# Gathering the first edge pass's rows of x during the first node pass, through a table by edge

## What is computed

```python
h = jnp.maximum(_layernorm(x, axis=-1), 0.0)
x = x + _L0_gnn_ref(src, dst, h, L0_gnn_W, L0_gnn_b)
h = jnp.maximum(_layernorm(x, axis=-1), 0.0)
x = x + _L1_gnn_ref(h, edge_index, edge_attr_4, edge_attr_16, ...)
```

```python
deg = 1.0 + jax.ops.segment_sum(jnp.ones((E,), X.dtype), col, num_segments=N)
dinv = jax.lax.rsqrt(deg)
XW = X @ W + b
scaled = XW * dinv[:, None]
msg = jax.ops.segment_sum(scaled[col], row, num_segments=N)
out = (msg + scaled) * dinv[:, None]
```

## Time and profile before

| what | value |
| --- | --- |
| median of three runs | 2155.31 us (2149.29 to 2168.29) |
| profiled execution, its own time | 2154.57 us |
| span in the profile | 2152.7 us |
| PE busy | 1692.0 us (79%) |
| VectorE busy | 1780.1 us (83%) |
| ScalarE busy | 1529.4 us (71%) |
| GpSimd busy | 1095.4 us (51%) |
| DMA moved | 437.75 MB, mean 203 GB/s |

### The profile page before, as it was taken

How to read it: one execution, slowest core, us unless ns; L and a number is a source line. 1 busy time by engine, 2 the same in 40 slices (tenths; PEclk the granted TensorE clock), 3 DMA queues, 4 the chain that set the end, 5 groups by cost and what they waited for, 6 DMA issues and landing times.

```text
span 2152.7 us, 53890 instructions
## 1 busy us (share of the span) xinstructions
PE 1692.0 (79%) x14246; PEld 1444.6 (67%) x14344; DVE 1780.1 (83%) x7827; ACT 1529.4 (71%) x3485; POOL 1095.4 (51%) x1065
## 2 busy tenths in 40 slices
PE   5979999999999798888578777679997777787100
PEld 3657888888888677777466666568885777777100
DVE  5778999999999688888488888779987999999664
ACT  3757788878788577877566666579996999999100
POOL 3105654455545577787567777744430222122576
PEclk9989999999999899999798999989998999999655
DMA  4689666666666577777456666567785888888784
GB/s 143 239 202 217 239 235 232 230 241 244 232 234 210 148 157 160 164 158 156 78 106 120 122 119 118 102 205 248 246 218 189 290 287 291 287 288 288 261 279 148
DMA packets 206640, 437.75 MB, mean 203 GB/s; under 512 B 49624, under 2 KB 87900, under 8 KB 206570
## 3 DMA queue, kind: packets, MB, share of 16 engines
q1 hardware_dynamic: 137018, 361.19, 49.2%
q0 software_dynamic: 56448, 74.95, 19.1%
q10 hardware_dynamic: 13104, 0.81, 1.5%
HBM read 220.18 MB, written 219.18 MB: 204 GB/s over the span
## 4 chain that ended last, share of the span: by engine, by line
PE 37%; issue 15%; ACT 13%; DMA 12%; POOL 10%; DVE 9%; SPq 1%; DVEq 1%; ACTq 0%; POOLq 0%
PE bank L817 15%; ACT hb L1087 7%; PE bank L797 6%; POOL big L503 4%; DMA big<-x_tab,idx 3%; DVE st L1349 2%; POOL msg_tab L514 2%; PE bank L776 2%; POOL x_tab L514 2%; DMA big<-in_x_dram,idx 2%; DMA out_dram<-osb,idx 2%; ACT ht L1236 2%; PE bank L813 2%; PE bank L938 2%; PE bank L948 2%
## 5 line engine op out<-in xcount | busy, mean ns | idle before, releaser
L1349 DVE BATCH_NORM_STATS2 st<-big 128x6 f32<-128x256 f32 x882 | 314.9, 413 | 87.8 <-DMA big<-x_tab,idx 65.4
L817 PE MATMUL bank<-w_sb,ht 128*128 128x256 f32 x1568 | 371.6, 380 | 9.8 <-issue 7.7
L817 PEld LDWEIGHTS bank<-w_sb,ht 128*128 128x128 f32 x1568 | 299.9, 191 | 47.5
L797 PE MATMUL bank<-ident,hb 128*128 128x128 f32 x1568 | 211.1, 278 | 89.6 <-ACT hb L1087 75.7
L503 POOL DMA_INDIRECT big<-x_tab,idx x196 | 193.1, 985 | 144.4 <-issue 51.9
L469 POOL DMA_INDIRECT node_edge<-node_tab,idx x196 | 188.3, 961 | 138.9 <-issue 50.6
L797 PEld LDWEIGHTS bank<-ident,hb 128*128 128x128 f32 x1568 | 178.3, 142 | 119.2 <-issue 83.6
L563 POOL TENSOR_TENSOR big<-big,bias 128x256 f32<-128x256 f32 x98 | 72.0, 734 | 324.1 <-ACT hb L1087 285.4
L1048 ACT ACTIVATE hb<-big,rs 128x256 f32<-128x256 f32 x392 | 207.5, 590 | 21.1 <-DVE rs L1372 21.1
L1087 ACT ACTIVATE hb<-big,rs 128x256 f32<-128x256 f32 x392 | 213.5, 591 | 4.0 <-DVE rs L1372 3.9
L1031 ACT ACTIVATE sd<-mv,eps_col 128x4 f32<-128x4 f32 (+1 forms) x343 | 103.2, 301 | 154.1 <-DVE mv L1358 153.8
(11 more groups left out here) (248 smaller groups left out, 4360.2 us busy)
## 6 DMA issues: line engine op xcount, KB each, us to landing
big<-in_x_dram SPq DMA_DIRECT2D x97, 512.0 KB, 4.2
x_tab<-x1b SPq DMA_DIRECT2D x97, 512.0 KB, 2.9
big<-x_tab SPq DMA_DIRECT2D x97, 512.0 KB, 4.2
out_dram<-x1b SPq DMA_DIRECT2D x97, 512.0 KB, 2.9
x_odd<-x1b SPq DMA_DIRECT2D x48, 512.0 KB
big<-x_odd SPq DMA_DIRECT2D x48, 512.0 KB
msg_tab<-zeros SPq DMA_DIRECT2D x50, 256.0 KB, 2.2
tpw_tab<-tpb SPq DMA_DIRECT2D x49, 256.0 KB, 2.0
```

The lines of the kernel that those rows point to most:

```text
L797: last = nc.tensor.transpose(bank[q][:, (2 * j + k) * P:(2 * j + k + 1) * P], hb[:, s.slot(2, 2), 2 * q + j, k * P:(k + 1) * P], ident[:])
L817: last = mm(y, ht[:, q, (2 * j + k) * P:(2 * j + k + 1) * P], w_sb[:, k, :], start=False, stop=(j == 1 and k == 1))
L1349: last = v.bn_stats(st[:, k, j, :], row)
```

## The change

All 98 gathers of x by `dst` move from the first edge pass into the first node pass. In GpSimd's stream each third small transfer is followed by one edge gather (`edge_row_step`), into `staged`, four slots of two columns that lie in `osb`; `pace` now counts four transfers to a group. SP's node pass gets a step skew of 12 instead of 4: in every even step from 12 on it waits for a pair of gathers and stores it to `edge_src`, a table of [49, 128, 512] float32. GpSimd waits before a pair until the pair four before it has been stored. When all are stored, SP's `odd_step` loads a step's rows from `edge_src` into `xg` as well, one plain DMA of 256 KB. In `e1_step` GpSimd keeps only the scatters, and its wait for the node pass in front of that stage is gone. Some semaphores are used again (`e3_got`, `ex_out`).

```diff
+        staged = osb[:].rearrange("p s i (a d) -> p (s i) a d", a=2)
...
-            def pace(n):
-
-                if n % 3 == 0 and n // 3 > 3:
-                    pool.wait_ge(p1["x1"].sem, 2 * (n // 3 - 3))
+            small = itertools.count()
+
+            def pace():
+
+                k = next(small)
+                if k % 4 == 0 and k // 4 > 3:
+                    pool.wait_ge(p1["x1"].sem, 2 * (k // 4 - 3))
+
+            others = itertools.count()
+
+            def edge_row_step():
+                k = next(others)
+                if k % 3 == 2:
+                    t = k // 3
+                    pair = Step(0, t // 2, t // 2, S, 4)
+                    if t % 2 == 0:
+                        landed(pool, edge_out, pair, 4)
+                    pace()
+                    pool.indirect_dma_start(staged[:, pair.slot(0, 4), t % 2, :], None, x,
+                                            rows_of(idx3[:, 1, t:t + 1])).then_inc(edge_got[pair.slot(0, 4)].sem, 16)
...
             def dst_step(s):
-                pace(s.k)
+                pace()
                 of_node_step(0, s.k)
+                edge_row_step()
...
             def list_step(s):
                 t = s.k
-                pace(T + 2 * t)
+                pace()
                 landed(pool, list_out, s, 1)
                 pool.indirect_dma_start(list_tab, rows_of(rank_i[:, t:t + 1]), idx3[:, 1, t:t + 1], None
                                         ).then_inc(list_out[0].sem, 16)
-                pace(T + 2 * t + 1)
+                edge_row_step()
+                pace()
                 of_node_step(1, t)
+                edge_row_step()
...
             def e1_step(s):
-                if s.live():
-                    gather(e1_got, s, 1, x, lambda s: done(pool, e1["relu"], s, 4))
                 if s.k == 4:
                     x1_landed(pool)
                 scatter_add(e1, e1_out, s, 4, x1_tab)
 
-            pool.wait_ge(p1["x1"].sem, 2 * (G - 4))
...
-            run_groups(sp, 4, p1_step)
+                if s.k >= 12 and s.even(12):
+                    pair = Step(s.b, (s.u - 12) // 2, (s.k - 12) // 2, S, 4, s.looped)
+                    landed(sp, edge_got, pair, 0, dmas=2)
+                    sp.dma_start(edge_src[pair.at()], staged[:, pair.slot(0, 4)].rearrange("p a d -> p (a d)")
+                                 ).then_inc(edge_out[pair.slot(0, 4)].sem, 16)
+
+            run(sp, G, 12, p1_step, first=2, unroll=XS)
...
+                    done(sp, e1["relu"], s, 4)
+                    sp.dma_start(xg[:, s.slot(0, 4)].rearrange("p a d -> p (a d)"), edge_src[s.at()]
+                                 ).then_inc(e1_got[s.slot(0, 4)].sem, 16)
...
             x1_landed(sp)
+            all_landed(sp, edge_out, S)
             run(sp, S, 0, odd_step)
```

More of the change, by code:

```diff
@@ L1 @@
+import itertools
 from contextlib import ExitStack
@@ L178, in build @@
         edge_x = dram("edge_x", [S, P, 2 * D])
+        edge_src = dram("edge_src", [S, P, 2 * D])
         x1_odd = dram("x1_odd", [S, P, J * D])
@@ L360, in build @@
         x_in, x1_out, list_out, node_in = sems("x_in", XS), sems("x1_out", 2), sems("list_out", 1), sems("node_in", 1)
+        edge_got, edge_out = sems("edge_got", 4), sems("edge_out", 4)
         e1 = named("e1", "own others chain_a chain_b chain_c eq sidx coef stats root norm relu turned ht xw v "
@@ L370, in build @@
         e3 |= after(e2, "stats root norm relu turned ht")
-        e3_got, eo_out, ex_out, msg_got = sems("e3_got", 4), sems("eo_out", 2), sems("ex_out", 4), sems("msg_got", 4)
+        e3_got = [Signal(one.sem, one.base + 32 * len(range(i, S, 4))) for i, one in enumerate(edge_got)]
+        eo_out, ex_out, msg_got = sems("eo_out", 2), reused(edge_out, S, 4), sems("msg_got", 4)
         fs = named("fs", "chain grams grams_end products z sums var root weights")
@@ L1530, in e1_step @@
                 if s.live():
-                    sums = edge_moments(e1, e1_got, s, 2)
+                    sums = edge_moments(e1, e1_got, s, 1)
                     mean_variance(e1, sums, "stats", 0, s.slot(0, 2), 2)
```

## The result

The changed kernel takes 2262.81 us in the median (2259.92 to 2268.62, four runs) against 2155.26 us of the kernel before: ratio 1.049, 95% interval 1.044 to 1.055. It is slower by 5%. The forecast was 2234 us, in a range of 2178 to 2300.

What follows compares the result with a forecast made beforehand. It took GpSimd's list scatters, each waiting for the last one's landing, to hold the path, and scatter landings as the edge pass's floor. 2154.6 + 79 (list) + 7 (handover) - 7 (edge pass) = 2233.6, said 2234 us; range 2178 to 2300.

Steps and rivals of the forecast that it cites:

- The list steps: GpSimd's list stage in the node pass: later start and longer steps move its end from 708.5 to 787.5 us, +79.
- delay of 1.0 us: List stage: added on each step with an edge gather, giving 4.89 us there and 4.55 in the mean.
- a gather just ahead: List stage: 1 KB rows queued ahead of the next list scatter make its landing up to 2.2 us later.
- the low end of 4.06: List stage: gather nearly hidden in the landing wait, 4.06 us a step; as rival 2192 us, chance 0.17.
- landings over 4 us in the median: List stage: sign that the forecast is right, with list steps of 4.5 us.
- SP and the node pass: Node pass: SP waits for gathered pairs; slack of 28 us is used up, then the pass slows to GpSimd's pace.
- DMA share of 0.85: Node pass: the added gathers and stores raise the DMA share from 0.68 by 0.17.
- Handover: From the list's last issue to the edge pass's first moments: 11.5 us instead of 4.6, +7.
- The floor: Edge pass: the chain scatter, landing, next scatter keeps a step at 6.49 us though the gathers leave GpSimd.
- my 7 us: Edge pass: gain from steps falling from 6.63 to 6.49 us, 0.14 us times 49; bounds 0 and 39.
- The rival that the gathers' going would give 39 us: Edge pass: steps fall to PE's 5.83 us; in rivals of 2123 us (chance 0.05) and 2149 us (chance 0.08).
- The added waits of SP: Edge pass: waiting for `relu` four steps back is covered, since a step is over 6 us; no cost.

Runs made afterwards that it cites:

- two_tables: load_first with list scatters going in turn to two tables, each waiting for the one two steps back, second table unread: 2155.63 us, ratio 1.0015.
- load_first: The changed kernel with SP's load of a step's edge rows moved in front of the wait for the odd group's relu: 2224.38 us, ratio 1.037.
- plain_one_scatter: plain_first with only the first of the two scatters of an edge step issued, half of the sums left out: 2121.52 us, ratio 0.989.
- plain_first: plain_behind with SP's load put in front of the odd group's wait: 2152.26 us, ratio 1.002 against the kernel before.
- plain_behind: Kernel before, node pass untouched; edge pass without gathers, SP loading sequential rows of x behind the odd load: 2174.76 us, ratio 1.013.

## Why the prediction was right, and where it was off

**The list steps.** Right in place and cause; the size of the sum came out too, though not its make-up. Forecast: start at 353 us, 4.55 us a step, 3.6 in the last twelve, last issue ending at 787.5 us. Measured: 354.1, 4.58 over the first 85, 3.50 after, 789.1. two_tables shows the wait for the landing to be the cause by taking it away. What the delay of 1.0 us was made of I had only partly right. I put it on steps with a gather, from queueing behind 1 KB rows and from traffic: 4.89 us with a gather, 3.86 without. Measured are 5.17 and 3.35, so the misses on the two kinds of step cancel in the mean, and that the sum is met within 2 us is in part luck; 1.0 was a choice near the middle between 0 and 2.2. The runs give: stores alone 0.34 us on each step, gathers alone 0.38, both 0.50 (load_first, 4.39), of which 0.22 the bytes of the gathers; the parts don't add up, since they hide in the same waits. Moving the gather away from the next scatter changed nothing for the better, so my picture of a gather just ahead is not borne out, and the low end of 4.06 isn't either: the mean was 4.45. I had tied that low end to the Trainium skill's rule (DMA: Bandwidth & Descriptors, Queues, rings and completion order), that an engine takes turns between queues, a whole packet at a time. That was a misreading: the gather and the list scatter both go through GpSimd's queue (q0 in the profile's table of queues), and the rule is on turns between different queues. It says nothing on how long one of them waits for the other. That the stores in SP's queue (q1) delay as much as the gathers speaks for the load of the DMA engines as a whole; it is argued, not shown. The sign "landings over 4 us in the median" is undecided: the view of `list_tab` gives 3.4, 3.6 and 3.8 us after (least, median, most), but the scatter at 521.29 us was waited for until 528.70, so that view doesn't cover them all.

**SP and the node pass.** Right: SP waited 204 us for gathered pairs, the node pass ran at GpSimd's pace in its second part, and the end of the list counted. The DMA share of 0.85 that I had worked out is there (0.83 and 0.84) as long as the node pass keeps its pace.

**Handover.** +7 forecast, +3.8 measured. The steps are those that I named, but the last gather landed 2.72 us after its start and SP's store in 2.00, where I had 3.7 and 3.6; the load took 3.98. The 3.6 us gained up to the first scatter I had not counted: before, VectorE stood 3.59 us before its moments at 719.30 us for gathered rows.

**The edge pass.** The floor was right: 6.49 us from one row, 6.56 and 6.58 in the two kernels that reach it, and a step near PE's 5.83 us only when the chain is cut (6.0 in plain_one_scatter). Even on this floor the gain is smaller than my 7 us: in plain_first the way from first to last scatter is 317.7 us against 319.4, 1.7 less. The rival that the gathers' going would give 39 us is refuted by plain_first. The failed step is the sentence on the added waits of SP: "The added waits of SP for `relu` four steps back are covered: that is the slot's old reader, and a step is over 6 us." I looked at the wait that the diff adds, and not at the one that already stood ahead of it in the same queue, `odd["relu2"]`. That is also four steps back by its index, but is given three steps later by ScalarE. The load moved from a queue without that wait to one with it. The term came out at +24.4 us where I had -7, 31 us off. With the list 2 us longer than forecast, and the handover and the start of the pass together 7 us shorter, that makes the 26 us between 79 forecast and 105 measured in the spans. load_first takes 25 us of it back, and plain_behind, the same order on the old kernel, takes 343.8 us from first to last scatter against 319.4, again +24. The time stayed inside the range because the range was wide for the list's sake, not because this term was seen.

**What stays open.** How the 0.50 us a list step divides between bandwidth and the number of transfers is known only in sums, from one trace each, and one trace of the unchanged list stage lies 0.19 us below the others. Whether SP's bursts make the long steps was not tried. No run that computes everything beat the kernel before: plain_first, which loads other rows, and two_tables, which leaves half of the list out, only equal it. A list in two tables would need a merge; that wasn't tried.

## What to carry to other kernels

When a load moves to another queue, go through every wait that already stands ahead of it there, and ask in which step of its engine the awaited signal is given, not how many steps back its index is. Idle time behind a serial chain of landings is not room: transfers put into it lengthened the landings themselves, and a chain one transfer deep carried each tenth of a microsecond on to the end of the stage; with two in flight all of it came back here. Before taking work off an engine that looks busy, find the rows where this work is already absent, here the last four pairs of the pass: they gave the step without it to 0.1 us.

## What the runs showed of the hardware that was not expected

The node pass kept its full pace with DMA at 0.84 and 282 GB/s. The landing of an accumulating scatter of 128 rows hardly cared for the traffic: 4.64 us to the next pair with hardly any other traffic (39 GB/s from 1032 to 1039 us), 4.67 in load_first beside 768 KB of loads a step. The small plain scatters into `list_tab` did care: their median rose from 3.4 to 3.9 us with 256 KB of stores per 11 us more, though the same code without these stores gave anything from 2.9 to 3.5 us in four traces.
